# Both expert passes of a graph-transformer layer in one loop, with the first sums in a table of their own

## The reference, cut to what matters

```python
xn = layernorm(x)                                   # x is (6250, 256)
x = x + graph_attention(xn, src, dst) + linear_attention(xn)
# mixture of experts on the normalised rows: 6 experts, each row takes the 2 best
features = layernorm(x)
rh = relu(features @ router_w1 + router_b1)
top_w, top_i = top_k(softmax(rh @ router_w2 + router_b2), 2)
routing_weights = softmax(top_w)
h1 = relu(features @ expert_w1[e] + expert_b1[e])   # 256 -> 256
h2 = relu(h1 @ expert_w2[e] + expert_b2[e])
expert_out = h2 @ expert_w3[e] + expert_b3[e]
out = x + sum over the 2 chosen e of routing_weights * expert_out
```

## Time and profile before

| | us |
|---|---|
| median of 3 runs | 796.24 |
| lowest, highest | 793.36, 800.51 |
| the profiled execution: its own time | 797.89 |
| its span, first to last instruction | 795.7 |
| TensorE busy in the span | 676.3 (85%) |
| VectorE busy | 559.5 (70%) |
| GpSimd busy | 402.5 (51%) |
| layer 1 of the first pair of pass 0 begins | 443.5 |
| layer 1 of the first pair of pass 1 begins | 620.7 |

### The profile page before, as it was taken

How to read it: one execution, slowest core, us unless ns; L and a number is a source line. 1 busy time by engine, 2 the same in 40 slices (tenths; PEclk the granted TensorE clock), 3 DMA queues, 4 the chain that set the end, 5 groups by cost and what they waited for, 6 DMA issues and landing times.

```text
span 795.7 us, 15452 instructions
## 1 busy us (share of the span) xinstructions
PE 676.3 (85%) x4744; PEld 622.7 (78%) x4744; DVE 559.5 (70%) x1399; ACT 443.0 (56%) x874; POOL 402.5 (51%) x443
## 2 busy tenths in 40 slices
PE   3878999999999888888850799999994899999992
PEld 2767788888888777777640699999994799999992
DVE  5674679888888757777645477777773477777772
ACT  2545566767777436677630555656651566565640
POOL 3455378876666000454536155555555155465553
PEclk9999999999999999999955799999998799999997
DMA  8885644444443445765324523443432535444420
GB/s 215 190 157 121 159 125 135 143 127 120 139 125 98 149 145 168 227 187 165 105 59 119 172 89 125 141 137 129 133 115 95 158 92 145 130 134 140 125 74 29
DMA packets 72463, 106.24 MB, mean 134 GB/s; under 512 B 24612, under 2 KB 45605, under 8 KB 72386
## 3 DMA queue, kind: packets, MB, share of 16 engines
q1 hardware_dynamic: 51074, 72.57, 32.4%
q0 software_dynamic: 21312, 32.69, 13.4%
HBM read 60.32 MB, written 46.78 MB: 135 GB/s over the span
## 4 chain that ended last, share of the span: by engine, by line
PE 76%; ACT 6%; DMA 5%; DVE 4%; issue 3%; POOL 3%; SPq 1%; POOLq 0%; DVEq 0%; ACTq 0%
PE kv_ps L1333 10%; PE kv_ps L1335 10%; PE kv_ps L1334 10%; PE pt L1325 6%; PE d_ps L1191 5%; PE kv_ps L1168 5%; PE kv_ps L1171 4%; PE kv_ps L1169 4%; PE kv_ps L1268 3%; PE xt_ps L1325 3%; DMA al_tab<-arena 2%; POOL tab L566 2%; PE pt L1259 2%; ACT staged L708 2%; PE pt L1168 2%
## 5 line engine op out<-in xcount | busy, mean ns | idle before, releaser
L1333 PE MATMUL kv_ps<-we_h,now_h 128*128 x648 | 197.3, 304 | 14.6 <-issue 7.2
L1335 PE MATMUL kv_ps<-we_h,now_l 128*128 x648 | 184.9, 285 | 0.0
L1334 PE MATMUL kv_ps<-we_l,now_h 128*128 x648 | 184.2, 284 | 0.0
L1333 PEld LDWEIGHTS kv_ps<-we_h,now_h 128*128 128x128 f32 x648 | 124.9, 193 | 20.2 <-issue 20.2
L1334 PEld LDWEIGHTS kv_ps<-we_l,now_h 128*128 128x128 f32 x648 | 124.7, 192 | 0.0
L1335 PEld LDWEIGHTS kv_ps<-we_h,now_l 128*128 128x128 f32 x648 | 124.2, 192 | 0.0
L1116 DVE TENSOR_TENSOR work<-kv_ps,be 128x256 f32<-128x256 f32 x216 | 81.7, 419 | 43.1 <-PE kv_ps L1335 43.0
L577 POOL TENSOR_TENSOR arena<-work,arena 128x256 f32<-128x256 f32 x80 | 53.1, 683 | 107.9 <-ACT work L745 107.9
L537 POOL DMA_INDIRECT alg<-al_tab,src_all x50 | 62.3, 1245 | 39.2 <-issue 24.9
L924 DVE TENSOR_REDUCE ss<-xring 125x16 f32<-125x1040 f32 x50 | 61.7, 1234 | 17.4 <-ACT xring L648 16.5
L760 ACT ACTIVATE now_h<-xt_ps 128x512 fp32r<-128x512 f32 x54 | 32.3, 599 | 69.3 <-PE xt_ps L1325 69.3
(11 more groups left out here) (239 smaller groups left out, 1823.7 us busy)
## 6 DMA issues: line engine op xcount, KB each, us to landing
arena<-tab SPq DMA_DIRECT2D x40, 259.0 KB, 3.0
xring<-in_x SPq DMA_DIRECT2D x26, 224.0 KB
xt_tab<-arena SPq DMA_DIRECT2D x10, 568.8 KB
arena<-tab SPq DMA_DIRECT2D x40, 131.0 KB, 2.1
we_h<-wt_h SPq DMA_DIRECT2D x6, 768.0 KB, 5.3
we_l<-wt_l SPq DMA_DIRECT2D x6, 768.0 KB, 7.7
weight_in<-tab SPq DMA_DIRECT2D x14, 259.0 KB, 2.9
xring<-in_x SPq DMA_DIRECT2D x5, 560.0 KB
```

The lines of the kernel that those rows point to most:

```text
L1333: pe.matmul(outp, hi[:, c, :], we_h[:, w], start=c == 0, stop=False)
L1334: pe.matmul(outp, hi[:, c, :], we_l[:, w], start=False, stop=False)
L1335: last = pe.matmul(outp, lo[:, c, :], we_h[:, w], start=False, stop=c == KC - 1)
```

## The change

Both passes become one loop over 54 pairs (`ALL`), `n` from -1 to 55, on every engine. For that, what pass 1 needs early is parted from what pass 0 makes late:

- `tab1` holds rows of 262 floats without a sum. `second_rows` on GpSimd scatters them straight from the row buffers, five pairs ahead of the sums (`AHEAD = 5`).
- The first sums go to a table `half` of their own (`put_half`), 256 floats each, from four new buffers `yw` (`YB = 4`), and come back by `load_half` on SyncE into the free half of the row buffer.
- Pass 0: ScalarE writes the scaled bias to `yw`, VectorE adds weight times product to it (`weighted`), and GpSimd scatters it. No addition on GpSimd.
- Pass 1: ScalarE writes the scaled bias, GpSimd adds the row to it (`residual`), VectorE adds weight times product, and one step later adds the first sum (`sums`); GpSimd scatters to `out` (`put_rows`).
- ScalarE's `third_bias` stands one step later for the same pair, in both passes.
- SyncE's fills of `tab1` and of `half` are two transfers where one was.

```diff
+ALL = 2 * PAIRS
+AHEAD = 5
+YB = 4
...
-        tab1 = nc.dram_tensor("tab1", (E * REG + S, ROW1), FP32, kind="Internal").ap()
+        tab1 = nc.dram_tensor("tab1", (E * REG + S, ROW), FP32, kind="Internal").ap()
+        half = nc.dram_tensor("half", (E * REG + S, D), FP32, kind="Internal").ap()
...
-            for j in range(-1, PAIRS + 2):
+            for n in range(-1, ALL + 2):
...
+            def load_rows(n):
+                k, j = n // PAIRS, n % PAIRS
+                for h in range(HB):
+                    first = sp.value_load(tab_row[0:1, k, j * HB + h:j * HB + h + 1], min_val=0, max_val=E * REG)
+                    if h == 0 and n >= U:
+                        sp.wait_ge(*emptied(n - U))
+                        if n - U < PAIRS:
+                            sp.wait_ge(*copied(n % U, n - U))
+                    if h == 0 and n == PAIRS:
+                        sp.wait_ge(tab_done, 2)
+                        sp.wait_ge(fill_out[1], 32 * (E + 1))
+                        for u in range(U):
+                            sp.wait_ge(*copied(u, PAIRS - 1))
+                    sp.dma_start(rb[n % U][:, h, D:ROW1], (tab0, tab1)[k][bass.ds(first, S), :]).then_inc(r_in[n % U], 16)
+            def load_half(n):
+                for h in range(HB):
+                    ...
+                    sp.dma_start(rb[n % U][:, h, 0:D], half[bass.ds(first, S), :]).then_inc(p_in[n % U], 16)
+            for n in range(ALL):
+                load_rows(n)
+                if n == U - 1:
+                    fill_up(1)
+                if n >= PAIRS + U - 1:
+                    while late < min(n - 3, ALL):
+                        load_half(late)
+                        late += 1
...
+            for n in range(AHEAD):                       # GpSimd
+                second_rows(n)
+            for n in range(PAIRS):
+                put_half(n)
+                if n + AHEAD < PAIRS:
+                    second_rows(n + AHEAD)
+            for n in range(PAIRS, PAIRS + 2):
+                residual(n)
+            for n in range(PAIRS, ALL):
+                if n + 2 < ALL:
+                    residual(n + 2)
+                put_rows(n)
...
+            def sums(n):                                 # VectorE
+                u = n % U
+                dve.wait_ge(p_in[u], 16 * HB * halves_in(n))
+                dve.wait_ge(y_done, (n + 1) * HB)
+                for h in range(HB):
+                    dve.tensor_tensor(rb[u][:, h, 0:D], yw[n % YB][:, h, :], rb[u][:, h, 0:D], ALU.add).then_inc(sum_done, 1)
...
+                if has(n - 1):
+                    dve.wait_ge(h2_h_done, n)
+                    dve.scalar_tensor_tensor(h2_l, th2_ps, 0.0, h2_h.bitcast(FP32), ALU.max, ALU.subtract).then_inc(h2_l_done, 1)
+                if has(n - 3) and n - 3 >= PAIRS:
+                    sums(n - 3)
```

More of the change, by code:

```diff
@@ L221, in gps_layer @@
         hs1, hs2 = rows_of(work, 0), rows_of(work, HB * F)
-        b3w = [rows_of(work, HB * F * (2 + b)) for b in range(2)]
+        yw = [rows_of(work, HB * F * (2 + b)) for b in range(YB)]
         b3_sb = xring[:, 0:E * D]
@@ L325, in expert_regs, with tiles, has, halves_in @@
             return [[engine.alloc_register(f"{name}{h}_{i}") for i in range(EL * HB)] for h in range(2)]
-        def tiles(engine, k, regs, step):
+        def tiles(engine, regs, step):
             es = {}
-            for j in range(-1, PAIRS + 2):
[L332 to L335, removed]
+            for n in range(-1, ALL + 2):
+                if has(n) and n % EL == 0:
+                    for i, e in enumerate(experts(engine, regs, n)):
+                        es[n + i // HB, i % HB] = e
+                step(n, es)
         def turn(n):
             return n // U
[L340 to L344, removed]
+        def has(n):
+            return 0 <= n < ALL
+        def halves_in(n):
+            return len(range(n % U + -(-(PAIRS - n % U) // U) * U, n + 1, U))
+        def emptied(n):
+            return z_out[n % U], 16 * HB * (turn(n) + 1)
+        def copied(u, n):
+            return second_out[u], 16 * HB * len(range(u, n + 1, U))
         block = ctx.enter_context(nc.Block())
@@ L448, in fill_up @@
                 tab = (tab0, tab1)[k]
-                rows = skip_rows[:, ROW1 - tab.shape[1]:ROW1]
+                rows = skip_rows[:, D:ROW1]
                 sp.load(end_regs, fill[0:1, k, 0:E])
@@ L484, in _ @@
+            late = PAIRS
+            for n in range(ALL):
[6 more added lines that the diff above has]
+                        late += 1
+            while late < ALL:
+                load_half(late)
+                late += 1
+            for n in range(ALL - U, ALL):
+                sp.wait_ge(*emptied(n))
         @block.gpsimd
@@ L768, in _ @@
+            normal(0)
+            tiles(act, act_e, step)
         @block.vector
@@ new lines, in plus_bias, with weighted @@
+            def plus_bias(rows, outp, layer, n, es, finished):
+                for h in range(HB):
+                    dve.tensor_tensor(rows[:, h, :], outp[:, h, :], be[layer][:, bass.ds(es[n, h] * F, F)], ALU.add).then_inc(finished, 1)
+            def weighted(n):
+                dve.wait_ge(l3_done, n + 1)
+                if n < PAIRS:
+                    dve.wait_ge(b3w_ready, (n + 1) * HB)
+                else:
+                    dve.wait_ge(xb_done, (n - PAIRS + 1) * HB)
+                for h in range(HB):
+                    w = D + C_W + n // PAIRS
+                    dve.scalar_tensor_tensor(yw[n % YB][:, h, :], l3_ps[n % 2][:, h, :], rb[n % U][:, h, w:w + 1], yw[n % YB][:, h, :],
+                                             ALU.mult, ALU.add).then_inc(y_done, 1)
@@ L1151, in _ @@
+            tiles(dve, dve_e, step)
+            sums(ALL - 1)
         @block.tensor
@@ L1373 @@
+            tiles(pe, pe_e, step)
 def kernel(**inputs):
```

270 lines of the change are left out of this document (120 added, 150 removed).

## The result

The changed kernel took **852.87 us** (median of 4 runs, 848.78 to 854.59), the kernel before 796.61 beside it: a ratio of 1.07, 95% interval 1.0663 to 1.0737. The profiled run has a span of 850.7 us against 795.7. The forecast was 792.

A forecast was written before the change was run, and what follows sets the result against it. TensorE was taken as the bound within a pass, the seam as the one large thing to win. Terms of -16.1 + 8 + 4 = -4.1 us from the median of 796.24 gave 792, range 783 to 803.

The forecast's parts named there:

- At nothing: Items priced at zero, among them pass 0: GpSimd's four scatters a step fill 5.4 us of 5.9.
- Rival C: Pass 0: GpSimd becomes the bound as the scatter pitch rises to 1.49 us; +5 us, 801; chance 0.09.
- E: Pass 1: scatter, rows and halves meet in the DMA queues, landings grow; +7 to +10 us, up to 806; chance 0.11.
- Term 1, the seam: Between the passes: 35.9 us shrink to three whole steps with registers, 18.3, plus 1.5 of waits; 16.1 us gained.
- Term 2, the ring: Row buffers in pass 1: scatter one step later, rows 1.65 us late; 8 us lost, 5 best, 19 worst.
- Term 3, registers on VectorE: `sums` delays VectorE's register loads and so the bias; priced at nothing beside the ring, by itself up to 3 us.
- Term 4, the end: Last pairs: third bias a step later delays the last `residual`, six scatters follow; 4 us lost.
- Rival D, contention: Pass 1: GpSimd and VectorE contend, all 0.76 us of `sums` on GpSimd's path to the scatter; +7, 799; chance 0.08.

The follow-up runs named there:

- e1: The changed kernel without `second_rows`, pass 1 reading its rows from `tab0`, so its values differ: 792.84 us, 0.997 of the kernel before.
- e14: e1 with `sums`, the halves' loads and the third bias one step earlier: 794.11 us, 0.9983 of the kernel before.
- e15: e14 with GpSimd's scatters also ahead of its additions in pass 1: 780.43 us, 0.9772 of the kernel before; pass 1 still reads pass 0's rows.
- e4: The changed kernel with expert registers loaded for nine pairs at a time instead of three (EL = 9): 810.72 us, 1.0147 of the kernel before.
- e6: The changed kernel with one more GpSimd addition of 128x256, result unused, after each `put_half`: 829.85 us, 1.0429 of the kernel before.
- e18: e1 with six idle copies behind every sixth `put_half`, a queue of eight scatters four times, ending about one step before register loads: 827.51 us.
- e9: The changed kernel with GpSimd's scatters ahead of its additions in pass 1 and the third bias at its old step: 850.74 us, 1.0651 of the kernel before.
- e5: e1 with one idle copy a pair, so three scatters a pair in pass 0: 790.92 us, 0.9925 of the kernel before.
- e2: The kernel before with two more scatters of 262 floats a pair in pass 0, into a spare table: 809.97 us, 1.0153 of the kernel before.

## Why the prediction was wrong

- **The step that failed** is "At nothing. Pass 0: GpSimd issues four scatters a step, 4 x 1.28 + 0.3 = 5.4 us of 5.9". The count, the pitch and the length of a scatter were right. What it left out is that unbroken scatters on GpSimd could cost the other engines time that GpSimd itself doesn't show: VectorE and ScalarE waited for semaphores of TensorE that came up to 6 us late. It was priced at 0 and measured 56.3, and e1 shows that it goes with the copies. What makes TensorE late stays open. Rival C asked after the pitch, which stayed; E after landings in pass 1; no rival had engines that stand still beside a full GpSimd. The trace before had queues of two and one of four in pass 0, and the long ones of L566 stood in another stage: four a step was outside of what it showed.
- **Term 1, the seam**: -14.2 against -16.1. Right. The three terms that were priced add up to +1.8 instead of -4.1. That e1, without the copies, comes to 792.84 beside the forecast's 792 is in part luck: its four stages differ from the kernel before by -2.9, -16.6, +13.2 and +6.0, nothing in sum, and the rest lies ahead of pair 0, where nothing changed.
- **Term 2, the ring**: +11.6 against 8, within its 5 to 19. The mechanism is the forecast's: ScalarE waits 34.4 us for rows, 18 times in 115 us. e14 and e15 show that one step earlier ends it.
- **Term 3, registers on VectorE**: priced at nothing beside the ring. In pass 0 of the changed kernel most long stalls stand right behind these loads, and they went with them in e4; but in e6 and e18 TensorE is late away from any load, so a part of the loads in the loss isn't shown.
- **Term 4, the end**: +4.4 against 4. e9, with the old place of the bias, has 35.1 instead of 37.9, but e5 has 33.1 with the new place, so the cause isn't shown.
- **Rival D, contention**: the price exists, its place was wrong. `sums` take 856 ns beside GpSimd's additions and 414 beside its scatters or nothing; GpSimd's additions take 753 in 700 to 780 where they took 683. The forecast's 0.1 came from L967 beside scatters, which is the one pairing without a price. The Trainium skill (GPSIMD Engine Reference, Key points) has the rule that VectorE instructions with two SBUF inputs contend with GpSimd: the trace agrees for GpSimd's additions, and not for its scatters. In the changed kernel it is hidden behind the late rows (e9 takes it away and the ring stage stays within what runs differ by); in e14 the additions' order, with the slow `sums` and the later scatter that come of it, keeps some 9 us (120.5 against 111.4).

## What to carry to other kernels

An engine with room in its busy share can still cost others time: before filling an engine's step with instructions of one kind, look whether the trace holds a queue of that length beside the same neighbours, and give the case a price where it doesn't. Where a wait has no named releaser, look up which instruction makes what is waited for, and compare its recorded end with the start of the one that waits: here that alone leads to TensorE. Where two late things end at the same place, taking one away shows nothing; try both together before dropping either. Work that only a seam needs is best added only ahead of it: six copied pairs won 7.8 of the 14.2 us that copying all 27 won there, without the 56.

## What the hardware showed that I had not expected

- Beside eight unbroken indirect scatters (1.29 us pitch) SyncE's instructions of 18 to 152 ns took about 700 ns, and at each queue one semaphore of TensorE came 5.6 to 6.4 us behind the recorded end of their matmuls, so that VectorE and ScalarE stood for up to 6.0 us, until 1.5 to 1.6 us after the last scatter. Beside fours this came in e6 (2.7 to 3.5 us late), and neither in e2 nor in e4.
- A VectorE addition of two 128x256 SBUF tiles: 414 ns alone or beside a scatter, 856 beside a GpSimd addition, which then takes 753 instead of 683.
- A load of 18 expert registers on VectorE (e4) lasted 1.6 to 4.8 us, one of 6 in the kernel before 0.8 to 1.4.
